# Linear attention of an adaLN block: positive part and high halves made by ScalarE, low halves one tile later

## The reference, cut to what matters

```python
qkv = jnp.einsum('bsd,de->bse', x, Wqkv) + bqkv
q, k, v = jnp.split(qkv, 3, axis=-1)
qp = jax.nn.elu(q) + 1.0
kp = jax.nn.elu(k) + 1.0
kv = jnp.einsum('bsd,bse->bde', kp, v)
num = jnp.einsum('bsd,bde->bse', qp, kv)
k_sum = jnp.sum(kp, axis=1)
den = jnp.einsum('bsd,bd->bs', qp, k_sum)[..., None]
attn = num / (den + ATTN_EPS)
x = layer_norm(x + attn, g1, b1)
```

## Time and profile before

| | us |
|---|---|
| median of 3 runs (lowest, highest) | 1055.07 (1054.29, 1056.33) |
| the profiled execution | 1054.94 |
| its span | 1053.0 |
| busy in the span: PE, DVE, ACT, POOL | 893.3, 754.5, 392.9, 415.1 |
| span of the stage, first to last product of TensorE before its output of the second batch row | 312.15 to 397.59 |

### The profile page before, as it was taken

One profiled execution on the slowest core, in us unless ns is written; L12 is line 12 of the kernel. 1 busy time (PEld: TensorE's weight loads), 2 busy tenths in 40 slices (PEclk: granted clock), 3 DMA queues, 4 the chain that ended last, 5 costly groups with the idle time before them and its releaser, 6 DMA issues. The chain is left out here.

```text
span 1053.0 us, 17851 instructions
## 1 busy us (share of the span) xinstructions
PE 893.3 (85%) x5616; PEld 762.5 (72%) x5616; DVE 754.5 (72%) x1450; ACT 392.9 (37%) x744; POOL 415.1 (39%) x480
## 2 busy tenths in 40 slices
PE   4399999999837775798875789977899999999998
PEld 1399999999835664587765655536578888888887
DVE  5888888888628787757775775625686777777676
ACT  4356666656414224222235345555711111111110
POOL 3177777877700133243451921310032332223322
PEclk9599999999959896799987899996999999999999
DMA  8336113244160000500000930000000101010002
GB/s 263 109 118 202 61 40 123 56 133 154 45 196 28 1 1 0 183 10 1 1 1 20 218 74 1 2 1 6 26 16 16 30 15 30 15 30 24 21 0 80
DMA packets 50299, 61.80 MB, mean 59 GB/s; under 512 B 8014, under 2 KB 37768, under 8 KB 50248
## 3 DMA queue, kind: packets, MB, share of 16 engines
q1 hardware_dynamic: 43464, 43.85, 13.2%
q0 software_dynamic: 6336, 17.31, 6.8%
q10 hardware_dynamic: 448, 0.01, 0.0%
HBM read 47.26 MB, written 7.60 MB: 52 GB/s over the span
## 5 line engine op out<-in xcount | busy, mean ns | idle before, releaser
L2023 POOL TENSOR_TENSOR e_hl<-e_h32sb,e_hh 128x512 fp32r<-128x512 f32 x68 | 88.1, 1296 | 270.3 <-DVE e_hh L2225 270.3
L2192 ACT ACTIVATE e_silusb<-psum 128x512 f32<-128x512 f32 x68 | 40.6, 598 | 240.2 <-PE psum L2079 240.2
L2307 DVE SCALAR_TENSOR_TENSOR y<-psum,comb,y 128x256 f32<-128x256 f32 x272 | 112.3, 476 | 0.1
L2222 DVE TENSOR_TENSOR e_h32sb<-psum,e_silusb 128x512 f32<-128x512 f32 x68 | 47.0, 692 | 74.2 <-PE psum L2079 60.4
L443 ACT ACTIVATE e_u<-psum,e_bias 128x256 f32<-128x256 f32 x152 | 63.7, 471 | 96.0 <-PE psum L342 88.2
L1883 DVE TENSOR_REDUCE at_mn<-psum 128x4 f32<-128x512 f32 x64 | 42.9, 688 | 25.5 <-PE psum L1555 25.2
L1290 POOL TENSOR_TENSOR ff_hl<-ff_h32sb,ff_hh 128x512 fp32r<-128x512 f32 x24 | 34.5, 1442 | 63.8 <-DVE ff_hh L1325 63.8
L2079 PE MATMUL psum<-act_hi,e_w0h 128*128 128x512 f32 x144 | 57.4, 398 | 0.3 <-ACT e_silusb L2192 0.3
L2079 PE MATMUL psum<-act_hi,e_w0l 128*128 128x512 f32 x144 | 56.8, 394 | 0.0
L2079 PE MATMUL psum<-act_lo,e_w0h 128*128 128x512 f32 x144 | 56.5, 392 | 0.0
L352 PE MATMUL psum<-e_w3h,e_h2h 128*128 (+1 forms) x160 | 47.9, 299 | 8.4 <-issue 8.0
(11 more groups left out here) (506 smaller groups left out, 3209.7 us busy)
## 6 DMA issues: line engine op xcount, KB each, us to landing
e_raw<-in_W SPq DMA_DIRECT2D x16, 512.0 KB, 6.7
e_raw<-in_W SPq DMA_DIRECT2D x8, 1024.0 KB, 5.9
y<-in_x SPq DMA_DIRECT2D x4, 512.0 KB, 9.4
v_tok<-in_xT SPq DMA_DIRECT2D x4, 512.0 KB, 8.0
y<-y_rows SPq DMA_DIRECT2D x4, 512.0 KB, 7.4
v_tok<-y_rows SPq DMA_DIRECT2D x4, 512.0 KB, 8.5
v_tok<-in_x SPq DMA_DIRECT2D x4, 512.0 KB, 8.8
e_raw<-in_w_gate SPq DMA_DIRECT2D x16, 128.0 KB, 2.1
```

Source lines behind the costliest of these rows:

```text
L2023: pool.tensor_tensor(hh[1][:, s % HS, :], h32[:, s % 2, :], hh[0][:, s % HS, :], ALU.subtract).then_inc(hsp, 1)
L2192: act.activation(sl_sb[:, s % 2, :], ps[s % 2][:, :], ACT.Silu).then_inc(esil, 1)
L2222: dve.tensor_tensor(h32[:, s % 2, :], ps[2 + s % 2][:, :], sl_sb[:, s % 2, :], ALU.mult).then_inc(h32d, 1)
L2307: dve.scalar_tensor_tensor(out=y[:, i, :], in0=ps[4 + j][:, 0:D], scalar=comb[:, i, bass.ds(2 * t + out_s // G, 1)], in1=y[:, i, :], op0=A ...
```

## The change

ScalarE takes over three things: the positive part of the keys (right after the exponential, in place), the high half of keys and values (`keys_hi`), and the high half of the queries (`query_hi`). VectorE keeps the sums and the low halves of the first eight tiles and the first four query halves, but makes each later: the low half of tile i - 2 stands at the head of iteration i, and the low halves of the queries stand behind the keys of the iteration that follows the group's first. GpSimd's part is the same. The instructions of TensorE are the same in the same order.

```diff
--- before.py
+++ after.py
@@ -939,7 +939,19 @@
                         act.wait_ge(kt, i + 1)
                         if i >= KS:
                             act.wait_ge(ksum, i - KS + 1)
-                        act.activation(ke_sb[:, i % KS, :], kv32[:, i % KS, 0:D], ACT.Exp).then_inc(ke, 1)
+                        act.activation(ke_sb[:, i % KS, :], kv32[:, i % KS, 0:D], ACT.Exp)
+                        act.activation(kv32[:, i % KS, 0:D], kv32[:, i % KS, 0:D], ACT.Relu).then_inc(ke, 1)
+
+                    def keys_hi(i):
+                        act.wait_ge(ksum, i + 1)
+                        if i >= 2:
+                            act.wait_ge(kvps, i - 1)
+                        act.activation(kt_s[i % 2][0][:, 0:2 * D], kv32[:, i % KS, :], ACT.Copy).then_inc(khi, 1)
+
+                    def query_hi(n):
+                        m, sl = split_at(n)
+                        act.wait_ge(qsum, n + 1)
+                        act.activation(qp[0][:, m, sl], qr_sb[:, n % 2, :], ACT.Copy).then_inc(qhi, 1)
 
                     act.wait_ge(bq_in, 16)
                     for i in range(NT):
@@ -951,8 +963,14 @@
                             for k in range(KC):
                                 hi(next_up(i - 1) * KC + k)
                         keys(i)
+                        if i:
+                            keys_hi(i - 1)
+                        if i % TG == 0:
+                            for k in range(KC):
+                                query_hi(g * KC + k)
                         if next_up(i):
                             halves(next_up(i))
+                    keys_hi(NT - 1)
                     for g in range(G):
                         act.wait_ge(rreq, g + 1)
                         act.activation(rstd[:, g * TG:(g + 1) * TG], rstd[:, g * TG:(g + 1) * TG], ACT.Sqrt).then_inc(root, 1)
@@ -1009,10 +1027,6 @@
                         dve.wait_ge(qact, n + 1)
                         dve.scalar_tensor_tensor(out=qr_sb[:, n % 2, :], in0=qe_sb[:, n % 2, :], scalar=1.0,
                                                  in1=qr_sb[:, n % 2, :], op0=ALU.min, op1=ALU.add).then_inc(qsum, 1)
-                        dve.wait_ge(qsum, n + 1)
-                        dve.tensor_copy(qp[0][:, m, sl], qr_sb[:, n % 2, :]).then_inc(qhi, 1)
-                        if n < NQ // 2:
-                            query_lo(dve, n)
 
                     def bias(i):
                         dve.wait_ge(kps, i + 1)
@@ -1024,15 +1038,8 @@
 
                         s_ = i % KS
                         dve.wait_ge(ke, i + 1)
-                        ch.link(dve.tensor_scalar(kv32[:, s_, 0:D], kv32[:, s_, 0:D], 0.0, None, ALU.max))
                         dve.scalar_tensor_tensor(out=kv32[:, s_, 0:D], in0=ke_sb[:, s_, :], scalar=1.0,
                                                  in1=kv32[:, s_, 0:D], op0=ALU.min, op1=ALU.add).then_inc(ksum, 1)
-                        dve.wait_ge(ksum, i + 1)
-                        if i >= 2:
-                            dve.wait_ge(kvps, i - 1)
-                        dve.tensor_copy(kt_s[i % 2][0][:, 0:2 * D], kv32[:, s_, :]).then_inc(khi, 1)
-                        if i < NT // 2:
-                            keys_lo(dve, i)
 
                     def finish(b):
 
@@ -1074,6 +1081,8 @@
                     dve.wait_ge(la_rin, 48)
                     for i in range(NT):
                         g = i // TG
+                        if 2 <= i < NB + 2:
+                            keys_lo(dve, i - 2)
                         if i % TG == 0:
                             for k in range(KC):
                                 query(g * KC + k)
@@ -1082,6 +1091,9 @@
                             finish(0)
                         if i:
                             keys(i - 1)
+                        if i % TG == 1 and i < NB:
+                            for k in range(KC):
+                                query_lo(dve, g * KC + k)
                         if i and next_up(i - 1):
                             for k in range(KC):
                                 lo(next_up(i - 1) * KC + k)
```

## The result

The changed kernel took 1064.45 us as the median of 4 runs (1063.55 to 1065.7) beside 1055.7 us for the kernel before: ratio 1.0088, 95% interval 1.0066 to 1.011. A ratio is not the quotient of the two medians, which is 1.0080 in the second comparison. So it is slower by 7 to 9 us.

The account below looks back on a forecast made before the run. VectorE's queue was taken to pace the first eight tiles, TensorE close behind, with handoffs deciding. Terms +2.9, +2.4, +2.8, -1.9 and -0.5 summed to +5.7 us, giving 1060.7 us, range 1058 to 1063.

Parts of the forecast that it names:

- VectorE idle before `combine` three times: Sign of being right: VectorE idles 1.5 to 3 us before `combine`, three times, with ScalarE's scalings as the cause.
- TensorE idle some 5 us in front of tiles 0, 3 and 7: Sign of being right: TensorE idles some 5 us before these tiles' products; 5.5 us walked for tile 0.
- a lone tile: Tile without other work, `bias(6)` to `bias(7)`: a ring through VectorE and ScalarE takes 2.7 us, 0.2 us slower than before.
- the first group: Up to `bias(4)`: scalings queue behind copies, `combine` and low half come late, TensorE's clock falls; +2.9 us, head's gain included.
- the second: Second group, `bias(4)` to `bias(8)`: later scalings and `combine`, slower lone tile, partly given back by the queries; +2.4 us.
- the third: Third group, `bias(8)` to `bias(12)`: transposes 3.5 us later, casts gone from VectorE give back 0.7; +2.8 us.
- the fourth: Fourth group, `bias(12)` to `bias(15)`: no `combine`, VectorE's shorter queue gains time; -1.9 us.
- to `finish(1)`: From `bias(15)` to `finish(1)`: ScalarE's copy is longer than the cast, but VectorE reaches the sum sooner; -0.5 us.
- after that nothing is changed, so the shift of `finish(1)` is the shift of the end: Behind `finish(1)`: claimed no further gain or loss, so the stage's +5.7 us carries to the end.
- No change: Rival: TensorE's clock stays up and scalings start earlier, each group keeps 1.3 us; sum 1.8 us, 1056.8 us; chance 0.15.
- Faster: Rival: only VectorE's queue matters and ScalarE's copies are always ready; -8 to -10 us, 1046 us; chance 0.10.
- More: Rival: lowered clock also in projections and queries, GpSimd's low halves on the fourth group's path; +9 to +11, 1065; chance 0.14.

Follow-up runs that it names:

- second comparison: Changed kernel, unedited, measured again on another occasion against the kernel before: 1063.25 beside 1054.77 us, ratio 1.0065.
- the wait: Changed kernel with GpSimd's last layer-norm addition waiting for VectorE's variance (L743): 1061.24 beside 1063.25 us without it; ratio to the kernel before 1.005.
- e4_warm: Changed kernel plus 30 unused transposes on TensorE before the waiting products in iterations 2, 5 and 9: 1057.63 us, ratio to the kernel before 1.003.
- e9: Changed kernel with ScalarE's scalings first, VectorE's low half ahead of combine, and two waits on GpSimd: 1054.45 us, ratio to the kernel before 0.9992.
- e8: Kernel before with keys' positive part and queries' high halves on ScalarE, query low halves later, two GpSimd waits: 1050.84 us, ratio to before 0.9955.

## Why the prediction was right and where it failed

**The direction and the mechanism were right.** VectorE idle before `combine` three times (1.95, 3.61, 3.61 us; the last two longer than the 1.5 to 3 given), TensorE idle some 5 us in front of tiles 0, 3 and 7, a lone tile at 2.6 us, no second table load: all there.

**The terms.** Taken from the stage's first product: the first group +2.6 us (forecast +2.9); the second +3.1 (+2.4); the third +3.5 (+2.8); the fourth -1.7 (-1.9); to `finish(1)` -1.2 (-0.5). Sum +6.3, forecast +5.7. That the sum is nearer than its terms is luck: their errors of -0.3, +0.7, +0.7, +0.2 and -0.7 cancel in part. The second group was under-sized mainly at one step: from the transposes to `bias(6)` I took the 3.9 us of before, but the way now leads through the exponential, positive part, high half and low half behind the transposed high halves (352.10 - 347.70 = 4.4). In the third the way to the transposes was 8.6 us instead of 8.4, 0.2 of it since `combine` met GpSimd (1.90 instead of 1.67 us), and behind them 0.2 us came back where I had counted on 0.7.

**The step that failed** is the sentence "after that nothing is changed, so the shift of `finish(1)` is the shift of the end". The instructions behind it are the same, but not their meeting: L743 and GpSimd's addition start within hundredths of each other, and their order turned over. The shift alone does not explain it, since both move with `finish(1)` (11.45 and 11.45 us behind it before, 11.43 and 11.41 now); what turned the order is not shown, and both profiles of the changed kernel without the wait have it. It costs 2.2 us in the profile and 2.0 us in the medians. I had given contention a place in the stage alone and priced it from there. Of the 4.7 us between the sum (5.7) and the profile (10.4), the rest is the terms' 0.6 and what lies outside the edits (0.7 ahead, 1.2 behind). For those last 1.9 us there was no experiment; profiles of one kernel differ by more, as told above. In the medians the miss is 3.75 us (1064.45 against 1060.7), of which the collision is 2.0 and the terms 0.6.

**The rivals.** *No change* needed the clock to stay up, and it did not. That the filler of `e4_warm` brought 3.7 us where the rival had 3.9 is a coincidence: the rival had 1.3 us in each group, the filler 0.2, 1.5 and 2.0. *Faster* is refuted for this order, and for the better one that was tried: `e9` only reaches the kernel before. *More* came nearest in size, by luck, with one cause right, the clock low into the projections (two of their products take 1.20 us at 349.26 and 370.78, 0.62 at the higher level), and one wrong: TensorE waits 3.1 us for GpSimd's low halves in the stage, against 5.9 before; what GpSimd cost more came behind the stage, by its addition.

The rule of the GPSIMD Engine Reference, section Specifications, of the Trainium skill, on contention with VectorE's instructions "in a 2-port perf mode or with two SBUF inputs", was named in the prediction for sums of two inputs. The rows agree for two inputs: `combine` takes 3.72 or 3.69 us beside GpSimd. L743 has one SBUF input and takes 2.38, and L1027, whose 1.387 us the prediction did price, has one too; whether it runs in a 2-port mode no run here shows.

## What to carry to other kernels

When work is handed to a less busy engine, look at what stands behind the new instructions in its queue and who waits for that; the busy shares of the engines say nothing of it. A wait that opens an idle stretch on TensorE can be paid twice, once in the stretch and once at the lower clock behind it. And two instructions can collide far behind the edit, where nothing was changed, so compare the small instructions of VectorE one by one beside each instruction of GpSimd, and pin the order with a wait where it hangs on hundredths.

## What was not expected of the hardware

A VectorE instruction of 128x4 took 2.38 us instead of 0.17 beside a GpSimd instruction of 128x1024 (2.37 us), while instructions with PSUM inputs were not held up: beside the same addition in the kernel before, the two low halves of 128x512 at 407.38 took 1.28 us together, as they do without GpSimd. Thirty transposes that compute nothing, 3.44 us each time, made a kernel 0.35 to 0.6% faster (1.003 against 1.0065 and 1.0088, compared across occasions). One of the nine runs of `e8` took 3002 us and was left out of the comparison; its cause is not known.
